# Preparing the last token groups and the router inside the first supersteps of the last layer

## The reference

```python
router_probs = softmax(x @ w_router)
gate_weights = softmax((x @ w_gating) / 0.1)
h = silu(x @ w_gate[e]) * (x @ w_up[e])          # e = 0..7, 256 -> 1024
expert_out[e] = h @ w_down[e]                    # 1024 -> 256
cw = router_probs * gate_weights
cw = cw / (cw.sum(-1) + 1e-9)
x = x + sum_e expert_out[e] * cw[:, e]
```

## Time and profile before

| | us |
|---|---|
| median of 3 runs | 1722.78 |
| lowest and highest of them | 1720.77, 1730.06 |
| the profiled execution, its own time | 1729.01 |
| its span, first to last instruction | 1727.2 |
| PE busy | 1592.0 (92%) |
| DVE busy | 1207.6 (70%) |
| ACT busy | 874.6 (51%) |
| POOL busy | 661.6 (38%) |

### The profile page before, as it was taken

One profiled execution on the slowest core, in us unless ns is written; L12 is line 12 of the kernel. 1 busy time (PEld: TensorE's weight loads), 2 busy tenths in 40 slices (PEclk: granted clock), 3 DMA queues, 4 the chain that ended last, 5 costly groups with the idle time before them and its releaser, 6 DMA issues. The chain is left out here.

```text
span 1727.2 us, 25997 instructions
## 1 busy us (share of the span) xinstructions
PE 1592.0 (92%) x7985; PEld 1289.0 (75%) x7986; DVE 1207.6 (70%) x2226; ACT 874.6 (51%) x1548; POOL 661.6 (38%) x585
## 2 busy tenths in 40 slices
PE   6998997779984888889999999999999999999998
PEld 5796673368882777768888888778788788788787
DVE  6656677736665789567677777767766776876875
ACT  4455332134432456555665665665655655656653
POOL 2542156688806634330540530521612603604500
PEclk9998898889995999889999999999999999999999
DMA  6994022168843212000100100101101101001001
GB/s 201 271 326 196 4 71 100 58 209 258 255 137 114 80 37 74 1 1 27 55 31 31 58 10 31 67 0 49 49 0 49 49 9 57 32 12 55 31 13 50
DMA packets 74493, 136.38 MB, mean 79 GB/s; under 512 B 8592, under 2 KB 52176, under 8 KB 74256
## 3 DMA queue, kind: packets, MB, share of 16 engines
q1 hardware_dynamic: 40544, 92.76, 16.4%
q10 hardware_dynamic: 27696, 25.51, 4.7%
q0 software_dynamic: 6144, 16.79, 3.1%
HBM read 90.93 MB, written 44.11 MB: 78 GB/s over the span
## 5 line engine op out<-in xcount | busy, mean ns | idle before, releaser
L1355 DVE TENSOR_TENSOR gU<-ps,gU 128x512 f32<-128x512 f32 x384 | 257.7, 686 | 78.3 <-PE ps L2565 67.3
L1348 DVE TENSOR_TENSOR eL<-eF,eH 128x512 fp32r<-128x512 f32 x256 | 191.9, 750 | 161.7 <-ACT eH L1828 161.7
L2041 POOL TENSOR_TENSOR cL<-cR,cH 128x384 fp32r<-128x384 f32 x192 | 211.8, 1129 | 241.5 <-ACT cH L1733 241.5
L1812 ACT ACTIVATE gU<-ps 128x512 f32<-128x512 f32 x384 | 225.7, 597 | 128.1 <-PE ps L2565 112.0
L1828 ACT ACTIVATE eH<-eF 128x512 fp32r<-128x512 f32 x256 | 161.2, 630 | 162.6 <-DVE eF L1343 162.1
L2565 PE MATMUL ps<-xTH,cH 128*128 128x512 f32 x512 | 204.2, 399 | 10.2 <-DVE eF L1343 5.9
L2565 PE MATMUL ps<-xTH,cL 128*128 128x512 f32 x512 | 202.1, 395 | 0.0
L2565 PE MATMUL ps<-xTL,cH 128*128 128x512 f32 x512 | 201.9, 394 | 0.0
L2585 PE MATMUL ps<-eH,cL 128*128 128x512 f32 x480 | 189.1, 394 | 0.0
L2585 PE MATMUL ps<-eH,cH 128*128 128x512 f32 x480 | 188.4, 393 | 0.0
L2028 POOL TENSOR_TENSOR cR<-cR 128x256 f32<-128x256 f32 x32 | 34.1, 1065 | 397.0 <-DMA cR<-in_w 397.0
(11 more groups left out here) (439 smaller groups left out, 3454.1 us busy)
## 6 DMA issues: line engine op xcount, KB each, us to landing
cR<-in_w SPq DMA_DIRECT2D x32, 768.0 KB, 4.1
slots_in<-eS SPq DMA_DIRECT2D x16, 768.0 KB, 10.4
eS<-in_wr SPq DMA_DIRECT2D x32, 384.0 KB, 4.3
xl<-slots_in ACTq DMA_DIRECT2D x48, 256.0 KB, 3.9
slots_out<-yo ACTq DMA_DIRECT2D x48, 256.0 KB, 3.2
cwB<-expert_weights SPq DMA_DIRECT2D x16, 512.0 KB, 3.4
k_parts<-parts SPq DMA_DIRECT2D x8, 512.0 KB, 5.5
q_parts<-parts SPq DMA_DIRECT2D x8, 512.0 KB, 3.9
```

Of the source, the lines that this page charges most:

```text
L1348: dve.tensor_tensor(eL[:, b, :], eF[:, b, :], f32(eH[:, b, :]), ALU.subtract).then_inc(block_low, 1)
L1355: dve.tensor_tensor(to[:, :], ps[:, 2 + half, :], to[:, :], ALU.add).then_inc(half_summed, 1)
L1812: act.activation(to[:, :], ps[:, half, :], ACT.Identity).then_inc(snap_done, 1)
L2041: last = pool.tensor_tensor(cL[c][:, cols_], cR[c][:, cols_], f32(cH[c][:, cols_]), ALU.subtract)
```

## The change

It does four things.

1. Group 2 is no longer prepared inside block B3. DVE's `spread` and `roots` of group 2 stand later in B3's list (`ffn_low` 1, then `spread`, then `ffn_low` 2, then `roots`), ACT normalises it behind B3's last activation, and PE turns it in superstep 0 behind P1, into banks 4 and 5. Group 3's `roots` moves behind `half_sum` 1 of superstep 0, its turn from the end of superstep 0 to superstep 1 (behind P1 and the first unit), and the six parts of `last_odd(3)` are spread over supersteps 1 to 3.
2. The router is made for each pair. Pair 0's `router_logits` moves from B3 to superstep 0 (between P7 and P5), pair 1's from superstep 2 to superstep 5. The exponential becomes two, in supersteps 1 and 5, each between `high_of(.., 1)` and `gate(.., 2)`. `router_weights` becomes two, at the ends of supersteps 1 and 5, and the transpose with its copy two, in supersteps 2 and 6.
3. SP stores and reloads the weights once for each pair, and its loop of chunk loads starts behind the second pair's.
4. The sums of the pairs (`tH`, `tL`, `tF3`), the router's scratch (`rt0`, `rt1`) and `cwT` stand at other SBUF addresses, and the router weights have another layout.

```diff
-        for p, off in enumerate((start["vext"], end["eS"] - 24 * 512)):
+        for p, off in enumerate((start["vext"] + LEAD, start["vext"] + LEAD + 32 * 512)):
...
-            sp.wait_ge(turned_copied, 5)
-            sp.dma_start(cw_d, cwT[:, :]).then_inc(cw_stored, 16)
-            sp.wait_ge(cw_stored, 16)
-            load_weights_of(0, 0)
-            sp.wait_ge(mix_read, 4)
-            load_weights_of(0, 1)
+            for p in range(2):
+                sp.wait_ge(turned_copied, 5 + p)
+                sp.dma_start(cw_d[64 * p:64 * p + 64], cwT[0:64, :]).then_inc(cw_stored, 16)
+                sp.wait_ge(cw_stored, 16 * p + 16)
+                wait(sp, mix_read, 4 * p)
+                load_weights_of(0, p)
...  DVE, block B3
             ffn_low("B", 3, 0)
             block_out("B", 2)
+            ffn_low("B", 3, 1)
             spread("L", 2)
+            ffn_low("B", 3, 2)
             roots("L", 2)
-            ffn_low("B", 3, 1)
-            ffn_low("B", 3, 2)
-            last_even(2)
             ffn_low("B", 3, 3)
-            router_shift(5, 0, 8, 1)
             block_out("B", 3)
...  DVE, superstep
                 if start:
-                    spread("L", 3)
+                    last_even(2, 4)
                 if first and s == 1:
                     last_odd(3, 0, 6)
-                    last_odd(3, 1, 6)
-                    last_odd(3, 2, 6)
-                if first and s == 2:
+                if first and s == 5:
                     router_shift(2, 8, 8, 2)
                 half_sum(e, s, 0, 0)
                 half_sum(e, s, 0, 1)
                 if start:
-                    roots("L", 3)
+                    spread("L", 3)
+                if first and s == 1:
+                    last_odd(3, 1, 6)
                 hidden(e, s, 0)
                 hidden_rest(e, s, 0)
-                if first and s == 1:
-                    last_odd(3, 3)
                 half_sum(e, s, 1, 0)
                 half_sum(e, s, 1, 1)
+                if start:
+                    roots("L", 3)
                 hidden(e, s, 1)
...
                 hidden_rest(e, s, 1)
-                if first and s == 1:
-                    last_odd(3, 4)
-                    last_odd(3, 5)
+                if start:
+                    router_shift(6, 0, 8, 1)
                 hidden(e, s, 2)
...
+                if first and s == 1:
+                    router_weights(0)
+                    last_odd(3, 2)
                 if first and s == 2:
-                    router_weights()
+                    last_odd(3, 3)
+                    last_odd(3, 4)
+                if first and s == 3:
+                    last_odd(3, 5)
+                if first and s == 5:
+                    router_weights(1)
...  ACT, block B3
             ffn_silu("B", 3, 0)
-            normalise("L", 2)
             ffn_silu("B", 3, 1)
             for part in range(3):
                 high(0, 1, part)
             ffn_silu("B", 3, 2)
-            turned("L", 2)
             ffn_silu("B", 3, 3)
             act.wait_ge(residual_added, 4)
+            normalise("L", 2)
...  ACT, superstep
+                if start:
+                    turned("L", 2, bank=4)
...
-                if first and s == 1:
-                    sums_of(1)
                 gate(e, s, 1)
                 high_of(e, s, 1)
+                if first and s in (1, 5):
+                    exponentials(s // 4)
+                if first and s == 2:
+                    sums_of(1)
                 gate(e, s, 2)
                 high_of(e, s, 2)
-                if first and s == 2:
-                    exponentials()
...  PE
-            block("B", 3, {3: ("L", 2)}, 5)
+            block("B", 3, {})
...
                 both("P1")
+                if start:
+                    pe.wait_ge(evac_done, 4 * (M_L1 - 1))
+                    turn("L", 2, bank=4)
...
+                units(0)
                 if first and s == 1:
                     pe.wait_ge(logits_read, 1)
-                units(0)
-                if first and s == 2:
+                    turn("L", 3, bank=6)
+                if first and s == 5:
                     pe.wait_ge(half_summed, 6 * s)
                     router_logits(2, 1)
-                if first and s == 3:
+                if first and s in (2, 6):
+                    p = s // 4
                     pe.wait_ge(half_summed, 6 * s)
-                    pe.wait_ge(cw_done, 1)
-                    pe.transpose(ps[:, 2, 0:P], cwc[:, :, :].rearrange("p e n -> p (e n)"), ident[:, :]).then_inc(turned_done, 1)
+                    pe.wait_ge(cw_done, p + 1)
+                    pe.transpose(ps[0:64, 2, 0:P], cwc[:, p, :, :].rearrange("p e n -> p (e n)"), ident[:, :]).then_inc(turned_done, 1)
...
                 both("P2")
                 both("P7")
+                if start:
+                    pe.wait_ge(evac_done, 4 * M_L1)
+                    router_logits(6, 0)
...
-                if start:
-                    pe.wait_ge(evac_done, 4 * M_L1)
-                    turn("L", 3, bank=6)
```

More of the change, by code:

```diff
@@ L42 @@
 STEPS = 2 * 4
+LEAD = 896
 PRODUCTS = ("P1", "P6", "P2", "P7", "P5", "P4", "P3")
@@ L97, in build @@
         cw2 = at("cw2", [P, NT, 16])
-        cwc = at("cwc", [P, E1, NT], F32, start["cw2"])
+        cwc = at("cwc", [P, 2, E1, 8], F32, start["cw2"])
         st = at("st", [P, NT, 6])
@@ L255, in build @@
         gU2 = [at(f"gU2{h}", [P, 512], F32, end["tL0"] + 2048 * h) for h in range(2)]
-        cwT = at("cwT", [P, P], F32, end["gU21"])
-        assert end["cwT"] <= end["vext"] and start["tH1"] >= end["vext"] and end["tL1"] <= end["eS"]
+        cwT = at("cwT", [P, P], F32, start["vext"])
+        assert end["cwT"] <= start["tH0"] and start["tH1"] >= end["gU21"] and start["tH1"] >= end["yg"] and end["tL1"] <= end["eS"]
         eH = at("eH", [P, 4, 512], F32R, start["sg"])
@@ L265, in build @@
         tm = at("tm", [P, 2, 512], F32, start["mx8"])
-        rt0 = at("rt0", [P, NT, 16], F32, start["mx8"])
+        rt0 = at("rt0", [P, NT, 16], F32, start["wk"])
         rt1 = at("rt1", [P, NT, 8], F32, end["rt0"])
-        assert end["tm"] <= start["idS"]
+        assert end["tm"] <= start["wk"] and end["rt1"] <= start["zcol"]
         ps = ctx.enter_context(nc.psum_tensor("ps", [P, 8, 512], F32))
@@ L546, in load_weights_of @@
             def load_weights_of(e, p):
-                rows = cw_d.rearrange("(e n) p -> e (n p)", n=NT)[:, p * 1024:(p + 1) * 1024]
+                rows = cw_d[64 * p:64 * p + 64].rearrange("(e n) p -> e (n p)", n=8)
                 src = rows[e:e + 1] if isinstance(e, int) else rows[bass.ds(e, 1)]
@@ L1199, in router_shift, with router_weights @@
                 dve.tensor_scalar(s1v[:, :, 1, :], s1v[:, :, 1, :], 10.0, None, ALU.mult).then_inc(shifted_done, 1)
[L1201 to L1212, removed]
+            def router_weights(p):
+                r = slice(8 * p, 8 * p + 8)
+                s1v = rt0[:, r, :].rearrange("p n (a e) -> p n a e", a=2)
+                dve.wait_ge(exp_done, 2 + p)
+                link(dve.tensor_reduce(sm[:, r, :], s1v, AXX, ALU.add))
+                link(dve.reciprocal(sm[:, r, :], sm[:, r, :]))
+                link(dve.tensor_tensor(s1v, s1v, sm[:, r, :].unsqueeze(3).to_broadcast([P, 8, 2, E1]), ALU.mult))
+                link(dve.tensor_tensor(rt1[:, r, :], s1v[:, :, 0, :], s1v[:, :, 1, :], ALU.mult))
+                link(dve.tensor_reduce(sm2[:, r], rt1[:, r, :], AXX, ALU.add))
+                link(dve.tensor_scalar(sm2[:, r], sm2[:, r], 1e-9, None, ALU.add))
+                link(dve.reciprocal(sm2[:, r], sm2[:, r]))
+                dve.tensor_tensor(cwc[:, p, :, :].rearrange("p e n -> p n e"), rt1[:, r, :], sm2[:, r].unsqueeze(2).to_broadcast([P, 8, E1]),
                                   ALU.mult).then_inc(cw_done, 1)
@@ L1455, in _ @@
                     acc = ps[:, 4 + 2 * j + t // 2, (t % 2) * D:(t % 2) * D + D]
-                    dve.scalar_tensor_tensor(x[:, tile, :], acc, cwc[:, E1 - 1, tile:tile + 1], x[:, tile, :], ALU.mult, ALU.add).then_inc(out_ready, 1)
+                    dve.scalar_tensor_tensor(x[:, tile, :], acc, cwc[:, 1, E1 - 1, tile - 8:tile - 7], x[:, tile, :], ALU.mult, ALU.add).then_inc(out_ready, 1)
         @block.scalar
@@ L1723, in _, with exponentials @@
                 weight_high("B", i)
-            def exponentials():
-                act.wait_ge(shifted_done, 3)
-                act.activation(rt0[:, :, :], rt0[:, :, :], ACT.Exp).then_inc(exp_done, 1)
+            def exponentials(p):
+                act.wait_ge(shifted_done, 2 + p)
+                act.activation(rt0[:, 8 * p:8 * p + 8, :], rt0[:, 8 * p:8 * p + 8, :], ACT.Exp).then_inc(exp_done, 1)
             def high(e, c, part):
@@ L1839, in superstep @@
                     turned_last(3, 6)
-                if first and s == 3:
-                    act.wait_ge(turned_done, 5)
```

(19 more changed lines are left out.)

11 lines of the change are left out of this document (8 added, 3 removed).

## The result

The changed kernel takes 1730.7 us (median of 22 runs, 1723.51 to 1736.74), the kernel before 1724.79 us (22 runs on the same chips). The ratio is 1.0034, with a 95% interval from 1.0023 to 1.0045: 5.9 us slower, within the 0.5% that the prediction took as no change, and 6.4 had been forecast. The size is right in part by chance: a gain that the prediction put at nothing offsets a cost that it put too low.

The account below looks back on a forecast made before the run. PE was taken to bound the last layer, losing 26.6 us before the change. After it, waits of 19.6 and half clock costing 13.4 make 33.0, 6.4 more; against the median 1722.8 that gives 1729 us, range 1717 to 1737.

Parts of the forecast that it names:

- no change: Whole kernel: a difference within about 0.5%, 8.6 us, can't be told from no change; given a chance of 0.57.
- The wait for POOL's sums: Block B3: ACT stands for POOL's sums of chunk 1, so PE waits 6.0 us for DVE's low part.
- the second: Block B3: PE waits 2.3 us before down 2 ends its gap to low part 3, which stands behind roots.
- P1's two halves: Start of superstep 1: PE waits 3.5 us before P1's first half and 1.5 before its second, 5.0 together.
- The router's half clock: Superstep 0: the router behind P7 lowers PE's clock to half for 6.7 us.
- Gate 2 behind the exponential: Supersteps 1 and 5: the exponential in front of gate 2 costs PE 0.7 us each time.
- the rival of the uncovered exponential: Supersteps 1 and 5: without cover all 2.9 us reach PE in place of 0.7, giving 1733 us; chance 0.03.
- The transposes: Supersteps 2 and 6: PE waits 2.0 and 1.9 us for the router weights.
- `last_odd` part 5: Supersteps 1 to 3: parts 3, 4 and 5 delay only hidden 3; taken at nothing, up to 2 us each uncovered.
- SP's queue: Superstep 7: chunk (1, 0) loads 6 to 8 us later at no cost; rival 3 us later still, 1731, chance 0.08.
- the slower rival: Supersteps 2 and 6: the clock also falls at both transposes, 1.7 to 2.9 us each, 1732 to 1735; chance 0.17.
- Addresses: Operations on tH or rt0 at other addresses in the same partitions: taken at 0, between -1 and +1 us.

Follow-up runs that it names:

- experiment 8: Changed kernel with the repairs of experiment 2, Experiment 3 and experiment 4, pair 0's transpose in superstep 3, last_odd part 5 earlier there: 1706.94 us, 0.9900 of the kernel before.
- experiment 2: Changed kernel with ACT's three pieces of high(0, 1) moved from block B3 into superstep 0: 0.9951 of the kernel before.
- Experiment 3: Changed kernel with group 3's roots back in front of hidden 0 of superstep 0 and pair 0's router_shift behind hidden_rest 2: 0.9988 of the kernel before.
- experiments 1 and 6: Kernel before: 1 with only tH, tL, tF3, cwT at the changed addresses, 0.9978; 6 with only last_odd(3)'s parts spread and sums_of(1) later, 0.9986.
- experiment 4: Changed kernel with both exponentials behind high_of(.., 2) instead of in front of gate 2: 0.9987 of the kernel before.
- experiment 5: Changed kernel with tH, tL, tF3 and cwT back at the addresses of the kernel before: 1.0058 of the kernel before.
- 9 to 11: Changed kernel with the pairs' sums at other starts, LEAD 1408, 1152 and 960 in place of 896: 1.0032, 1.0026 and 1.0060 of the kernel before.

## Why the prediction was right, and where it was not

**Block B3: mechanism right, size short.** The wait for POOL's sums was put at 6.0 and was 6.7; the second at 2.3 and was 3.7. The term that was mis-sized is roots: 4.1 us was taken from the earlier trace rows, 6.0 was measured. The prediction took the 4.1, read beside POOL's sums, for a place where POOL was in `chunk_rest`. In experiment 8 roots has only sums beside it:

```profile
687.51 0.70 DVE L1091 TENSOR_SCALAR vA<-mv 128x4 f32<-128x4 f32 x1
...
691.08 0.16 DVE L1108 SCALAR_TENSOR_TENSOR ofs<-mv,scl 128x4 f32<-128x4 f32 x1
```

That is 3.7 us, as in experiment 2, and the wait is 2.5 there and 2.7 in experiment 2. The half clock was put at 8.2 us and was 6.7.

**Superstep 0: right.** 3.5 and 1.5 were forecast in front of P1's two halves, 4.1 and 0.9 came, 5.0 both ways. Experiment 3 shows that the two edits named are the cause together. The router's half clock was put at 6.7 us, as the kernel before has it, and was 3.3. That isn't chance alone: it was 3.3 to 3.5 us in all nine traces that have the full router in superstep 0. But the 6.7 of the router in B3 was one execution's, since experiments 1 and 6, with the same router in the same place, have 3.4.

**Supersteps 1 to 3 and 5 to 6: two terms short, one missed.** Gate 2 behind the exponential was put at 0.7 each time and was 2.05 and 0.48; experiment 4 shows that the exponential's place is the cause. Superstep 1 has parts of `last_odd` and POOL's work beside it (hidden 1 took 1.32 us for 0.69), superstep 5 has neither, so the cover of 2.4 us, read in a superstep without them, was there in the one and mostly gone in the other; this reason is read from the traces and not tried. It is the rival of the uncovered exponential, in part and at one of its two places, for which the prediction gave 0.03. The transposes waited 1.56 and 1.58 for 2.0 and 1.9 forecast, and the copy cost 0.2 for 0.7. `last_odd` part 5 was taken at nothing ("delay only hidden 3") and cost 1.7: the step that failed is "whose unit comes a superstep later". P1 of superstep 4 itself waits for `pair_ready`, which this operation signals, and it stood at the very end of superstep 3. Experiment 8, with this part moved forward, doesn't have the wait. The bound of up to 2 that stood beside it held.

**SP's queue: no cost, as forecast, but the delay was larger.** Chunk (1, 0)'s sums began at 835.83, 10.9 us later than in the earlier trace rows. Counted from the first mark it is 16.5 us, of which 8.55 are the growth of the stretch itself; 6 to 8 were forecast. The sums ended at 839.4 and ACT took them up at 841.01 without a wait. The margin was 1.6 us.

**The clock at the transposes: right.** It didn't fall, and the slower rival didn't happen.

**Addresses: wrong.** 0 between -1 and +1 was forecast. Measured were -2.9 us in six experts, which makes -3.9 for all eight by my estimate, shown by experiments 1, 5 and 9 to 11. "No row distinguishes addresses" was true of the rows read, but the start-to-start times of the traces, taken by operand, distinguish the two kernels.

**The sum.** The reordered stretch was put at +6.4 and took +8.55. Inside it the waits were 3.7 us longer than forecast (23.3 for 19.6) and the half clock cost 2.0 less (11.4 for 13.4). The addresses were put at 0 and gave -3.2 outside it. The net of about +5 agrees with the measured 5.9 because these errors have opposite signs, and that is luck. By the order alone the kernel is 0.58% slower (experiment 5, 0.37 to 0.78), which by its middle is outside the prediction's "no change" though inside its range.

## What to carry to other kernels

A wait that is taken off one engine is worth what the next instruction in each list lets through. Here ACT's 7 us behind group 2's norm hid 7 us behind POOL's sums, and the gain came when both had moved (experiment 2). Moving the second alone wasn't tried. Work put in front of an operation that releases the bottleneck's next step (gate 2, hidden 2) must fit into the cover of that very superstep, with everything else that the change adds to it; the same work a place later costs little (experiments 3, 4 and 8). A stretch of half clock read in one execution isn't the price of its place: with the same code it was 6.7 us in one and 3.4 in two others. And where data is laid out anew, compare times by operand: here starts at a multiple of 256 bytes in the arena took the least time, and they gave back about four tenths of what the order cost.

## What the runs showed of the hardware that was not expected

With the moving operands of three products in seven (`tH`, `tL`) 64 bytes, or 128 and 704 bytes, behind a multiple of 1024, six experts took 737.2 to 737.4 us; with 0, 256 or 512 bytes 734.3 to 734.9. In the kernel before these 864 matmuls took 2.9 ns more from start to start than in the changed one, which is 2.5 of the 2.94 us; with 64 bytes they have only about half of it. Offsets count from the start of the kernel's arena, which begins at byte 16512 of the partition, 128 behind a multiple of 1024. Counted from the start of the partition, the starts with the shorter time are 128 bytes behind a multiple of 256 and the others 0, 64 or 192. So the runs show which starts take less time, and not that alignment is the reason. Whether the effect is of the moving operand's reads or of something else at these addresses wasn't tried: the high and low parts and `gU2` moved together.

The narrow router matmuls bring the clock to half while PE is never idle: in superstep 5 it was at 1.00 before them, fell 2.9 us behind the first of them (800.75) and stood at 0.50 for 7 us, and it stayed at 1.00 when there were six of them in place of 40. How long it stays down differs: behind the router of superstep 5 it was 6.8 to 7.0 us in seven traces and 3.4 in two, those of experiments 4 and 8. The changed kernel's waits of 2.1, 1.6 and 1.7 us between stretches of wide matmuls didn't bring the clock down, those of 6.7 us and of 4.1 with 0.9 did. The length of the wait alone doesn't decide it: one of 2.0 us at 678.3 in the kernel before was followed by 3.4 us at 0.50, and in block B3 the 2.7 us of experiment 2 brought it down and the 2.5 of experiment 8 did not. What decides wasn't isolated.

The ten small dependent operations of roots took 1.9 us alone and 3.7 to 4.1 beside POOL's sums, where four or five of them took 0.57 to 0.70 in place of 0.16. With POOL's low parts beside the first three, which took 0.92 to 0.96 each, and its sums beside the rest, it was 6.0.
